# The fifteen middle passes of a fused transformer layer: a loop on the engines, or written out

## The chip, the cores and the metric

The kernel runs on one core of a Trainium2 chip. The metric is the time of one execution on the device, in microseconds (us), as the median of several runs.

## The reference

One pre-norm transformer layer on x of shape (16, 512, 256), f32, batch B = 16:

```
x = x + attn(layernorm(x))          # causal, ALiBi bias, 32 query heads, 16 key/value heads, head dim 64
x = x + ffn(layernorm(x))           # U1: 256->64, V1: 64->1024, gelu(tanh form) + b1, U2: 1024->64, V2: 64->256, + b2

qkv = x @ W_qkv                     # W_qkv (256, 4096)
scores = q @ k.T / 8 + slope * (pos_k - pos_q), masked where pos_q < pos_k
out = softmax(scores) @ v ; out @ W_out      # W_out (2048, 256)
```

## The kernel before

Every f32 product is made from f16 halves: a value is kept as hi + lo, and a product is three matmuls (lo times hi, hi times lo, hi times hi). Line numbers are those of the profile (L445 is the helper that issues nearly all matmuls).

**Tiling.** One batch element (512 tokens, 4 tiles of 128) is one unit of work. For it the kernel goes through 16 steps s, one for each key/value head, and each step has 5 segments n = 0 to 4. In each segment TensorE does a block of scores, a block of scores for the row maxima, and in fixed segments a projection of q, k or v, the product of probabilities and v (L445, o_acc), a piece of the output projection (proj from wo), transposes, and pieces of the feed-forward part.

**Stages.** The work of one head is spread over later steps: projections in step s, maxima 2 steps later, exponentials 7 later (ATT = 7), the product with v 8 later, the output projection 12 later, then the second layernorm and, in steps 13 to 15, the feed-forward part of the element before. So the body for index i holds the front of element i and the tail of element i - 1.

**Modes.** The body is a Python function that each engine builds for itself. It is built three times: as FIRST (i = 0, without the tail), as MID (i = 1 to 15, everything), and as LAST (i = 16, only the tail). FIRST and LAST are straight code with counts that are Python integers. MID is built once and stands in a loop on each engine (`eng.Fori(1, B)`, L340), run 15 times: 14 times the branch at its end is taken, once it falls through into LAST.

**Waits.** Engines are tied together only by semaphores that count up over the whole kernel and are never reset, so each wait needs a count that grows with i. A count is an object `Count`: i times a factor plus a constant. The function `at` turns it into what the wait takes: outside the loop an integer; in the loop a register. At the top of the loop each engine multiplies i by nine factors (`MULTIPLES`); where the constant isn't zero, `at` issues a `reg_add` on that engine right ahead of the wait (L327), into one register named target. There is no barrier between the engines at the loop's end: each has its own loop and its own branch, and only the counts hold them together.

**Order.** The order of each engine's instructions is written out by hand in tables (`FFN_PAIRS`, `X_PAIRS`, `U1_AT`, `LN2_AT` and so on). What stands around the end of a pass is, on TensorE: the last scores of step 15, the last maxima, the transposes of the next element's x (L462), the last product of the feed-forward part (`ffn_y`: proj from v_hi and h), then at the top of the next pass the first scores of step 0, maxima, transposes of o (L567). On ScalarE (ACT) p_hi (L696) and the exponentials p_f (L738); on GpSimd (POOL) p_lo = p_f - p_hi (L1090); on VectorE (DVE) the masked row maxima (L925), the hi/lo remainders (L851), and the sums into x_rows (L1032). SyncE (SP) issues the DMAs that copy the q and k halves into the layout the matmuls read, and those of x and of the result.

Of the kernel before, what the change touches and what calls it, by code (L numbers as in the profile page):

```python
# [154 lines left out]
MULTIPLES = (1, 2, 4, 8, 16, 32, 64, 80, 192)  # L155
# [4 lines left out]
FIRST, MID, LAST = "first", "mid", "last"  # L160
# [55 lines left out]
def layer(nc, x, w_qkv, w_out, u1, v1, b1, u2, v2, b2, k_aug, q_aug, ident_d, ident_b_d, causal_d, out):  # L216
    B = x.shape[0]
    ctx = ExitStack()
    with ctx:
# [115 lines left out]

        def iterations(name, eng, body):
            body(Count(0), FIRST)
            regs = {n: eng.alloc_register(f"{name}_{n}") for n in (*MULTIPLES, "target")}
            regs["eng"] = eng
            with eng.Fori(1, B) as i:  # L340
                for times in MULTIPLES:
                    eng.reg_mul(regs[times], i, times)
                body(Count(i, regs), MID)
            body(Count(B), LAST)


# [4 lines left out]
        def _(sp):  # L351
# [28 lines left out]
            def body(i, mode):  # L380
# [47 lines left out]
                if mode != FIRST:  # L428
                    sp.wait_ge(y_done, at(2 * i + FREE))
                    sp.dma_start(out[(i - 1).value()].rearrange("(t p) d -> p t d", p=P), x2[:, :, :]).then_inc(y_out, 16)  # L430

            iterations("sp", sp, body)
            sp.wait_ge(y_out, 16 * B + FREE)
            sp.wait_ge(x_in, 16 * (B + 1))
# [3 lines left out]
        def _(pe):  # L438
# [31 lines left out]
            def body(i, mode):  # L470
# [171 lines left out]
                for s in range(KV):  # L642
# [8 lines left out]
                    for n in range(SEG):  # L651
# [35 lines left out]
                        if (s, n) in U2_PAIRS and mode != FIRST:  # L687
                            ffn_u2(U2_PAIRS[s, n])

            iterations("pe", pe, body)  # L690


        @block.scalar
        def _(act):
# [30 lines left out]
            def body(i, mode):  # L725
# [39 lines left out]
                for s in range(KV):  # L765
# [3 lines left out]
                    for n in range(SEG):  # L769
# [67 lines left out]
                        if (s, n) in U1_AT and mode != FIRST:  # L837
# [4 lines left out]
                            copy(pp[0:RANK, t * P:(t + 1) * P], proj("p", t)[0:RANK, 0:P], 1.0 / FFN_SCALE).then_inc(hi_pp, 1)  # L842

            iterations("act", act, body)


# [331 lines left out]
```

## Time and profile before

| | us |
|---|---|
| median of 3 runs | 3042.26 (3040.5 to 3043.39) |
| profiled execution, its own time | 3041.37 |
| its span, from first to last instruction | 3039.6 |
| PE busy | 2813.3 (93%) |
| DVE busy | 2194.7 (72%) |
| ACT busy | 2190.9 (72%) |
| POOL busy | 1730.0 (57%) |

PE is TensorE's matmuls and PEld its weight loads; a busy share is of the span. Register, branch and semaphore instructions are not counted as busy, so the work that the loop itself makes shows only as idle time of the engines, put down to "issue" where no semaphore explains it, and in the answer for a source line, which counts such instructions too (PEldq, ACTq, DVEq, POOLq, SPq are the engines' sequencers).

### The profile page before, as it was taken

Reading aid. Unit: us, or ns where it says so; the run is one execution under the profiler, and the core shown is the slowest. Engines: PE = TensorE matmul, PEld = TensorE weight load, DVE = VectorE, ACT = ScalarE, POOL = GpSimd, SP = SyncE. Lnnn points to the kernel's source line nnn. Section 1 sums busy time; section 2 is a strip of 40 time slices with the busy share of each in tenths; the row PEclk is TensorE's granted clock in tenths of the full one; section 3 lists DMA queues with packets and bytes.
Section 4 is the critical chain, followed back from the end, with each engine's and each line's share of the span. In section 5 each row is a group of like instructions: output and inputs, shape, how many; then the busy total and the mean of one; then the engine's idle time right before and its main releaser. Section 6 shows DMA issues by size and latency. Waiting matters only on the chain.

```text
span 3039.6 us, 99681 instructions
## 1 busy us (share of the span) xinstructions
PE 2813.3 (93%) x32328; PEld 1966.0 (65%) x32328; DVE 2194.7 (72%) x6987; ACT 2190.9 (72%) x3892; POOL 1730.0 (57%) x1560
## 2 busy tenths in 40 slices
PE   4999999999989999999999999999899999999986
PEld 1666675766757666676666767667676666767664
DVE  6777677776767777677776777767677776777763
ACT  3767777777777777777777777777777777776783
POOL 1555565555655656555565665556555555565664
PEclk9999999999999999999999999999999999999998
DMA  5332232322223222232322323222232322323210
GB/s 169 68 72 58 63 71 46 79 58 69 62 55 77 53 72 60 56 76 49 78 58 60 73 47 79 55 72 60 56 75 50 77 59 56 73 48 82 55 35 8
DMA packets 220087, 195.25 MB, mean 64 GB/s; under 512 B 41738, under 2 KB 217866, under 8 KB 219274
## 3 DMA queue, kind: packets, MB, share of 16 engines
q1 hardware_dynamic: 219540, 188.32, 26.3%
q8 instruction: 299, 4.90, 0.7%
q14 instruction: 248, 2.03, 0.2%
HBM read 27.73 MB, written 8.39 MB: 12 GB/s over the span
## 4 chain that ended last, share of the span: by engine, by line
PE 31%; issue 27%; POOL 27%; ACT 5%; DVE 3%; POOLq 1%; ACTq 0%; DVEq 0%
POOL p_lo L1090 26%; PE proj L445 13%; PE scores L445 7%; PE o_acc L445 6%; PE max_scores L445 2%; PE ffn_acc L445 2%; ACT h_f L824 1%; ACT L738 1%; DVE v_lo L851 1%; ACT p_f L738 1%; ACT L824 1%; POOL h_lo L1113 1%; PE transposes L567 1%; DVE max_scores L925 1%; POOLq L327 1%
## 5 line engine op out<-in xcount | busy, mean ns | idle before, releaser
L1090 POOL TENSOR_TENSOR p_lo<-p_f,p_hi 128x512 f16<-128x512 f32 x1280 | 1476.6, 1158 | 1073.3 <-ACT p_hi L696 1070.8
L738 ACT ACTIVATE p_f<-scores 128x512 f32<-128x512 f32 x1280 | 756.4, 591 | 333.9 <-PE scores L445 211.5
L696 ACT ACTIVATE p_hi<-p_f 128x512 f16<-128x512 f32 x1280 | 802.3, 627 | 48.0 <-issue 33.7
L925 DVE CUSTOM_DVE_ANT_0 max_scores<-max_scores,causal 128x384 f32<-128x384 f32 (+3 forms) x1184 | 564.1, 508 | 274.6 <-PE max_scores L445 265.3
L445 PE MATMUL scores<-q_hi_lo,k_lo_hi 128*128 128x512 f16 (+3 forms) x2048 | 613.1, 300 | 28.4 <-issue 28.0
L445 PE MATMUL scores<-q_hi_aug,k_hi_aug 128*128 128x512 f16 (+3 forms) x2048 | 585.7, 299 | 0.0
L445 PE MATMUL o_acc<-v_hi_one,p_lo 128*128 128x65 f16 x5120 | 517.6, 194 | 13.7 <-POOL p_lo L1090 13.7
L445 PE MATMUL o_acc<-v_hi_one,p_hi 128*128 128x65 f16 x5120 | 517.9, 194 | 0.0
L445 PE MATMUL o_acc<-v_lo,p_hi 128*128 128x64 f16 x5120 | 517.7, 193 | 0.0
L445 PEld LDWEIGHTS o_acc<-v_hi_one,p_lo 128*128 128x128 f16 x5120 | 471.7, 98 | 49.7 <-issue 12.8
L445 PEld LDWEIGHTS o_acc<-v_lo,p_hi 128*128 128x128 f16 x5120 | 468.4, 98 | 19.5
L445 PEld LDWEIGHTS o_acc<-v_hi_one,p_hi 128*128 128x128 f16 x5120 | 468.6, 97 | 0.0
L445 PE MATMUL scores<-ident_bf,causal 128*128 128x128 bf16 x2048 | 448.0, 219 | 0.0
L925 DVE CUSTOM_DVE_ANT_0 ffn_acc<-ffn_acc,causal 128x384 f32<-128x384 f32 (+2 forms) x864 | 413.4, 509 | 26.3 <-PE ffn_acc L445 25.1
L445 PE MATMUL max_scores<-k_hi_aug,q_hi_aug 96*128 96x384 f16 (+3 forms) x1184 | 282.8, 300 | 52.1 <-DVE row_max L925 48.8
L445 PE MATMUL proj<-xn_t_hi,wqkv_lo 128*128 128x512 f16 x768 | 293.7, 382 | 28.8 <-DVE v_lo L851 27.3
L445 PE MATMUL proj<-xn_t_hi,wqkv_hi 128*128 128x512 f16 x768 | 292.8, 381 | 0.0
L445 PE MATMUL proj<-xn_t_lo,wqkv_hi 128*128 128x512 f16 x768 | 292.7, 381 | 0.0
L925 DVE DVE_READ_ACCUMULATOR2_ANT row_max<- 128x1 f32 x2048 | 284.4, 139 | 1.3
L445 PE MATMUL proj<-wo_hi,o_t_lo 128*128 128x256 f16 x1024 | 280.7, 274 | 2.6 <-DVE o_t_lo L851 1.5
L445 PE MATMUL proj<-wo_hi,o_t_hi 128*128 128x256 f16 x1024 | 280.3, 274 | 0.0
L445 PE MATMUL proj<-wo_lo,o_t_hi 128*128 128x256 f16 x1024 | 280.2, 274 | 0.0
(115 smaller groups left out, 5205.9 us busy)
## 6 DMA issues: line engine op xcount, KB each, us to landing
q_hi_aug<-q_pair_hi SPq DMA_DIRECT2D x512, 64.0 KB, 2.0
q_hi_lo<-q_pair_hi SPq DMA_DIRECT2D x512, 64.0 KB, 2.1
q_hi_lo<-q_pair_lo SPq DMA_DIRECT2D x512, 64.0 KB, 2.0
k_hi_aug<-k_pair_hi SPq DMA_DIRECT2D x256, 64.0 KB, 2.0
k_lo_hi<-k_pair_hi SPq DMA_DIRECT2D x256, 64.0 KB, 2.0
k_lo_hi<-k_pair_lo SPq DMA_DIRECT2D x256, 64.0 KB, 2.2
x_rows<-in_L_attn_inputs SPq DMA_DIRECT2D x17, 512.0 KB, 3.7
x_residual<-in_L_attn_inputs SPq DMA_DIRECT2D x16, 512.0 KB, 3.7
```

The source lines that it names most:

```text
L327: count.regs["eng"].reg_add(count.regs["target"], count.regs[count.times], count.plus)
L445: return nc.tensor.matmul(out_ap, lhs, rhs, start=start, stop=stop, skip_group_check=True)
L567: last = nc.tensor.transpose(bank[:, qt * P:(qt + 1) * P], o_f[:, qt, :], ident[:, :])
L696: return nc.scalar.activation(out_ap, in_ap, ACT.Copy, scale=scale)
L738: nc.scalar.activation(p_f[:, k % 3, :], score_bank[k % 2][:, :], ACT.Exp).then_inc(exp_done, 1)
L824: nc.scalar.activation(h_f[:, c % 2, :], proj("h", c)[:, :], ACT.Gelu_apprx_tanh, bias=b1c[:, c:c + 1], scale=1.0 / FFN_SCALE).then_inc(ge ...
L851: return nc.vector.scalar_tensor_tensor(out=out_ap, in0=bank, scalar=scale, in1=high, op0=ALU.mult, op1=ALU.subtract)
L925: last = nc.vector.tensor_tensor_reduce(out=bank, in0=bank, in1=causal[:, (T - 1 - qt) * P:S], scale=1.0, scalar=-3e38, op0=ALU.add, op1=A ...
L1090: nc.gpsimd.tensor_tensor(p_lo[:, slot, n, :], p_f[:, k % 3, :], p_hi[:, slot, n, :], ALU.subtract).then_inc(lo_p, 1)
L1113: nc.gpsimd.tensor_tensor(h_lo[:, c % 2, :], h_f[:, c % 2, :], h_hi[:, c % 2, :], ALU.subtract).then_inc(lo_h, 1)
```

## The change

The loop on the engines goes. The MID body is built fifteen times, one after the other, with i as a Python integer. `Count` then has no registers, so `at` gives an integer in each wait, no `reg_add` and no `reg_mul` is issued, and the addresses of the DMAs of x and of the result are constants. The order of the instructions in a body, the tiles and the semaphores stay as they are.

```diff
         def iterations(name, eng, body):
             body(Count(0), FIRST)
-            regs = {n: eng.alloc_register(f"{name}_{n}") for n in (*MULTIPLES, "target")}
-            regs["eng"] = eng
-            with eng.Fori(1, B) as i:
-                for times in MULTIPLES:
-                    eng.reg_mul(regs[times], i, times)
-                body(Count(i, regs), MID)
+            for i in range(1, B):
+                body(Count(i), MID)
             body(Count(B), LAST)
```

## Rows read from the trace of the kernel before

**Rows 1.** The page: its head, busy slices and granted clock.

```profile
PE 2813.3 (93%) x32328; PEld 1966.0 (65%) x32328; DVE 2194.7 (72%) x6987; ACT 2190.9 (72%) x3892; POOL 1730.0 (57%) x1560
...
PEclk9999999999999999999999999999999999999998
```

**Rows 2.** Waits of PE, whole span: total us, times, longest us.

```profile
PE max_scores L445 <- DVE row_max L925: 48.8, 39, 2.6
PE scores L445 <- issue: 28.0, 14, 2.4
PE proj L445 <- DVE v_lo L851: 27.3, 32, 1.2
```

**Rows 3.** Waits of PE in one pass, 723.5 to 907 us.

```profile
PE max_scores L445 <- DVE row_max L925: 2.7, 2, 1.4
PE scores L445 <- issue: 2.3, 1, 2.3
PE proj L445 <- DVE v_lo L851: 1.7, 2, 1.2
PE proj L445 <- DVE k_pair_lo L851: 1.2, 1, 1.2
PE proj L538 <- DVE v_lo L851: 0.8, 1, 0.8
PE proj L538 <- ACT h_f L824: 0.6, 1, 0.6
PE o_acc L445 <- POOL p_lo L1090: 0.4, 1, 0.4
PE proj L445 <- DVE x_acc L932: 0.3, 1, 0.3
```

**Rows 4.** Timeline around the third loop edge, PE, ACT, POOL, DVE: start, duration.

```profile
720.65 0.27 PE L445 MATMUL proj<-v_hi,h_hi 128*128 128x256 f16 x1
723.23 0.39 PE L445 MATMUL scores<-q_hi_lo,k_lo_hi 128*128 128x512 f16 x1 [2.30 <-issue]
...
719.65 0.60 ACT L696 ACTIVATE xn_t_hi<-transposes 128x512 f16<-128x512 f32 x1
722.77 0.63 ACT L696 ACTIVATE p_hi<-p_f 128x512 f16<-128x512 f32 x1 [2.52 <-issue]
...
723.47 1.16 POOL L1090 TENSOR_TENSOR p_lo<-p_f,p_hi 128x512 f16<-128x512 f32 x1 [4.78 <-ACT p_hi L696]
...
720.89 1.28 DVE L1032 SCALAR_TENSOR_TENSOR x_rows<-proj,x_rows 128x512 f32<-128x512 f32 x2
724.55 0.70 DVE L925 CUSTOM_DVE_ANT_0 max_scores<-max_scores,causal 128x512 f32<-128x512 f32 x1 [2.38 <-PE max_scores L445]
```

**Rows 5.** Line L340 (loop head and branch): count, min/median/max ns, first and last start.

```profile
L340 PEldq FUSED_REGOPS  x15: 84/84/88, 168.2 to 2747.6; - x15
L340 PEldq COMPARE_BRANCH  x15: 76/3684/4062, 350.5 to 2928.0; - x15
```

**Rows 6.** PE's timeline where the loop is left, after its 15th pass.

```profile
2929.74 0.27 PE L445 MATMUL proj<-v_hi,h_hi 128*128 128x256 f16 x1
2929.85 0.38 PE L445 MATMUL scores<-q_hi_lo,k_lo_hi 128*128 128x512 f16 x1
2930.06 0.22 PE L445 MATMUL scores<-ident_bf,causal 128*128 128x128 bf16 x1
2930.12 0.38 PE L445 MATMUL scores<-q_hi_aug,k_hi_aug 128*128 128x512 f16 x1
2930.34 0.38 PE L445 MATMUL max_scores<-k_hi_aug,q_hi_aug 96*128 96x512 f16 x1
2930.56 0.60 PE L567 MATMUL transposes<-ident,o_f 128*128 128x128 f32 x4
2930.99 0.38 PE L445 MATMUL scores<-q_hi_lo,k_lo_hi 128*128 128x512 f16 x1
```

**Rows 7.** PE's timeline: first scores of passes 2 and 15, each after a loop edge.

```profile
354.88 0.39 PE L445 MATMUL scores<-q_hi_lo,k_lo_hi 128*128 128x512 f16 x1 [2.35 <-issue]
...
2747.82 0.39 PE L445 MATMUL scores<-q_hi_lo,k_lo_hi 128*128 128x512 f16 x1 [2.28 <-issue]
```

**Rows 8.** PE's timeline where the loop is entered from FIRST.

```profile
169.44 0.38 PE L445 MATMUL scores<-q_hi_lo,k_lo_hi 128*128 128x512 f16 x1
...
170.28 0.39 PE L445 MATMUL max_scores<-k_hi_aug,q_hi_aug 96*128 96x512 f16 x1 [0.19 <-DVE row_max L925]
171.09 0.65 PE L567 MATMUL transposes<-ident,o_f 128*128 128x128 f32 x4 [0.43 <-DVE xn_t_lo L851]
```

**Rows 9.** Line L327 (the reg_add ahead of a wait), by engine.

```profile
L327 PEldq ALU_OP  x5445: 32/32/42, 168.6 to 2927.5; - x195
L327 ACTq ALU_OP  x5400: 35/35/38, 169.9 to 2928.2; - x193
```

**Rows 10.** Line L736 (a second wait, outside the loop only).

```profile
L736 ACTq EVENT_SEMAPHORE  x92: 17/17/17, 85.7 to 2981.2; - x92
```

**Rows 11.** PE's timeline: start of steps 13 and 14 in FIRST, 5 and 6 in pass 3.

```profile
136.92 0.38 PE L445 MATMUL scores<-q_hi_lo,k_lo_hi 128*128 128x512 f16 x1
...
146.80 0.38 PE L445 MATMUL scores<-q_hi_lo,k_lo_hi 128*128 128x512 f16 x1
...
590.00 0.38 PE L445 MATMUL scores<-q_hi_lo,k_lo_hi 128*128 128x512 f16 x1
...
599.87 0.38 PE L445 MATMUL scores<-q_hi_lo,k_lo_hi 128*128 128x512 f16 x1
```

**Rows 12.** DMA queues in one pass, 539.64 to 724 us: packets, MB, share.

```profile
q8 instruction: 18, 0.29, 0.7%
q14 instruction: 16, 0.13, 0.2%
```

## The prediction

> **What bounds the kernel now.** I read the page first, then the waits of PE, then the timeline where a pass of the loop ends, then the two source lines that the loop makes (L340, L327), which the page doesn't count as busy. The page shows PE busy for 93% of the span, every other engine at 72% or less, and a granted clock of nine tenths or more, so the 2.4 GHz level, in nearly all slices [rows 1]. PE sets the pace, and what counts is what its idle time waits for. In the list of its waits one entry belongs to no engine: 28.0 us in 14 times, put down to issue, ahead of the first scores of a pass [rows 2]. Fourteen is the number of times that the loop's branch is taken. In a single pass that wait is there once (2.3 us), beside 7.7 us of waits for DVE, ACT and POOL, about ten of them (2.7 + 1.7 + 1.2 + 0.8 + 0.6 + 0.4 + 0.3) [rows 3].
>
> The timeline shows the edge itself [rows 4]. PE's last matmul of the pass starts at 720.65 and the first of the next at 723.23. ACT stands still for 2.52 us at the same place, also with issue named, and POOL and DVE then wait for these two. Nothing in the data holds PE there: the scores follow at once where the loop is left. L340 says what does: PE's compare-and-branch takes 3684 ns as a median and 76 ns at the least, the one time that it falls through [rows 5]. PE has matmuls queued when its sequencer stands at the branch, which is why 3.7 us of branch leave some 2.0 us of idle PE.
>
> **The change, part by part.**
>
> *The branch.* It goes, 14 times. What comes in its place is the code as it now runs from pass 15 into LAST: the last projection at 2929.74, the scores at 2929.85, 0.11 us later, and then maxima, transposes and the next scores at 2930.34, 2930.56 and 2930.99 with no wait named before any of them [rows 6]. That is the closest row to what every edge becomes, and it has the same feed-forward tail before it. Two ways to price the 14 edges. By the idle row: 28.0 us. By the length of passes: from the first scores of pass 2 (354.88) to those of pass 15 (2747.82) are 13 passes with an edge each, (2747.82 - 354.88) / 13 = 184.07 us; from there to the first scores of LAST (2929.85) is one pass without a taken edge, 182.03 us [rows 7 and 6]. The difference is 2.04 us, and 14 x 2.04 = 28.6 us. I take 28.6.
>
> *What is late next.* In the gap DVE does its last two sums into x_rows, 720.89 to 722.17 [rows 4], and the next pass's second block of maxima and its q projection wait for them. Without the edge PE starts the scores at about 720.76. In the exit the second scores start 1.14 us after the first and are some half a microsecond long [rows 6], so PE comes to these maxima about 1.6 us after 720.76, at 722.4: after DVE, by 0.2 us. ACT can do p_hi at 720.25 instead of 722.77, when its last copy ends, and POOL follows it. So I take no new wait. The other end is the entry from FIRST, also without an edge ahead: there DVE and the o transposes are late by 0.19 and 0.43 us as named [rows 8], and that pass lasts 354.88 - 169.44 = 185.44 us against 184.07, so 1.37 us more [rows 7 and 8]. FIRST ends without the feed-forward tail, which is PE's time for the others to catch up, so it is the farther row; I keep 14 x 1.37 = 19.2 us as the upper price of a give-back.
>
> *The register instructions.* 5445 of them on PE at 32 ns and 5400 on ACT at 35 ns [rows 9], and in each pass the multiplications at the top, behind the branch (the fused pair on PE takes 84 ns) [rows 5], which lies inside the edge that I have priced. If every reg_add of PE stood bare on its path it would be 5445 x 0.032 = 174 us. It doesn't: steps that do the same in FIRST, with constants, and in the loop, with registers, take the same time, 146.80 - 136.92 = 9.88 us for step 13 of FIRST and 599.87 - 590.00 = 9.87 us for step 5 of pass 3 [rows 11]. Where PE has matmuls queued the sequencers' work is hidden by them, and a step is unchanged to 0.01 us, over 240 steps at most 2.4 us either way. What is left are the ten waits of a pass outside the edge, where PE has run dry and the chain over ACT or DVE counts. A reg_add of about 35 ns in it goes, but where it also carried a first wait, a semaphore instruction stands in its place (17 ns on ACT [rows 10]). Say 18 ns net for each of ten waits: 0.18 us a pass, 2.7 us in 15. The ends are nothing (or 2.4 us lost), and three instructions of 35 ns in each wait with nothing in their place, 10 x 3 x 0.035 x 15 = 15.8 us. I take 3 us, near the lower end because the semaphore instruction is the near row.
>
> *Fetching the longer program.* I take nothing. One pass already brings 18 and 16 packets of instructions over its two queues [rows 12]: the body is fetched afresh in every pass, so writing it out fetches the same amount, in order. Within a pass PE has no wait for issue but the one at the edge [rows 3].
>
> At this place the Trainium skill bears on the sum twice. "Runtime: NRT & Kernel Launch", section on instruction fetch mechanics, says that fetching in order is mostly hidden and that a taken branch to a place out of the buffered window stalls; this trace agrees, with 3684 ns for the taken branch and 76 ns for the other. "Advanced Engine Details and Errata", section Control Flow Timing, gives a compare-and-branch about 108 ns; by that figure 14 branches would be an estimated 1.5 us, and the trace's 28.0 us would have to be something else.
>
> *The DMAs.* SP issues the same ones, with constant addresses. It isn't waited for by PE in a pass [rows 3], so no gain and no loss.
>
> **Sum.** 3041.37 - 28.6 - 3 = 3009.8 us for the profiled execution. It is 0.9 us below the median of the runs (3042.26), so about 3010.5 for a median; I say 3010.
>
> **The rivals.** A measurement of this kernel can tell about 0.2% (6 us) from no change.
>
> - *Give-back at the seam.* The edge goes, but it has been the pause in which DVE and ACT caught up, and PE waits for them in step 0 as at the entry: 28.6 - 19.2 = 9.4 us, and 3 for the registers: 3042.3 - 12.4 = 3030. For it: the entry rows. Against it: the exit, which has no such wait, and the 0.2 us that I find in hand.
> - *The stall isn't the branch.* Some other thing between passes costs the 2 us and stays (a wait across engines that the trace can't see); then only the branch's own 76 ns and the registers go: 14 x 0.076 + 3 = 4 us, 3038. For it: issue only means that nothing visible explains it. Against it: two engines stop at once, the minimum of 76 ns is the fall-through, and PE flows on there.
> - *Slower: straight code comes late.* Fetching 15 bodies in order misses now and then, each miss at the price of an edge, 2.0 us of idle PE. There are 18 packets on the larger queue in a pass, 270 in 15. If one in ten missed, 27 x 2.0 = 54 us: 3042 - 32 + 54 = 3064. It decides from 32 / 2.0 = 16 misses on. For it: a loop could prefetch something a long program doesn't. Against it: inside the pass the same 18 packets come with no such wait.
> - That the change doesn't do what it says I leave at nothing: with integers `at` can't issue a register instruction.
>
> **How the numbers follow.** My forecast 85%, the give-back 8%, the stall that isn't the branch 4%, slower 3%. The forecast itself runs from 2998 (15.8 for the registers instead of 3) to 3016 (2.4 lost there instead of 3 won). The give-back lies at 3030; I go a part of the way to it, to 3020, since a small give-back of 0.3 us an edge (4 us) is within what I can't exclude, and leave its full size outside. Faster by over 0.2%: the forecast and the give-back, 0.93; the same, 0.04; slower, 0.03.
>
> **What would show it.** The trace after should have no register or branch instruction on the five queues but a last one of SP; no wait of PE for issue at the first scores of a pass; p_hi of ACT at the seam without its 2.5 us; passes of 181.5 to 182.1 us from first scores to first scores. Step 5 of a pass should stay at 9.87 us. The waits of PE outside the edge should stay near 7.7 us a pass, and a little less would be the register part. The prediction is wrong if waits for DVE or ACT of a microsecond stand in step 0 of each pass (give-back), or if waits for issue of about 2 us are strewn over the passes (fetching).

## The result and the profile after

| | before | after |
|---|---|---|
| median, us | 3042.82 | 3003.11 (3001.69 to 3005.99) |
| ratio to before | | 0.9865, 95% interval 0.9853 to 0.9877 |
| profiled execution, us | 3041.37 | 3001.69 |
| its span, us | 3039.6 | 2999.9 |
| instructions in the trace | 99681 | 85467 |

The kernel is 1.35% faster, 39.7 us. I forecast 3010 (2998 to 3020). (The median before is now one of four runs, hence 3042.82 and not 3042.26.) The first lines of the page after answer to [rows 1]:

```profile
span 2999.9 us, 85467 instructions
...
PE 2804.2 (93%) x32328; PEld 1970.4 (66%) x32328; DVE 2203.5 (73%) x6987; ACT 2194.3 (73%) x3892; POOL 1726.2 (58%) x1560
...
q8 instruction: 257, 4.21, 0.6%
q14 instruction: 151, 1.24, 0.1%
```

The same 32328 matmuls; PE's busy time is 9.1 us less (0.3%) and its idle time 30.6 us less. The two queues that bring instructions carried 257 and 151 packets. PE's waits over the whole span, to set beside [rows 2] (us in total, times, longest):

```profile
PE max_scores L441 <- DVE row_max L921: 52.6, 40, 2.7
PE proj L441 <- DVE v_lo L847: 27.3, 32, 1.2
PE proj L441 <- DVE k_pair_lo L847: 18.5, 15, 1.2
```

The entry "PE scores <- issue: 28.0, 14" is gone and has no successor. (Lines after are 4 lower than before: L441 is L445, L921 is L925.) The timeline at the seam of passes 3 and 4, as in [rows 4]: start, duration, for PE, then ACT, POOL and DVE.

```profile
712.65 0.27 PE L441 MATMUL proj<-v_hi,h_hi 128*128 128x256 f16 x1
712.76 0.38 PE L441 MATMUL scores<-q_hi_lo,k_lo_hi 128*128 128x512 f16 x1
713.90 0.38 PE L441 MATMUL scores<-q_hi_lo,k_lo_hi 128*128 128x512 f16 x1
...
711.65 0.60 ACT L692 ACTIVATE xn_t_hi<-transposes 128x512 f16<-128x512 f32 x1
712.14 0.62 ACT L692 ACTIVATE p_hi<-p_f 128x512 f16<-128x512 f32 x1
713.45 0.60 ACT L734 ACTIVATE p_f<-scores 128x512 f32<-128x512 f32 x1 [0.68 <-PE scores L441]
...
712.84 1.16 POOL L1086 TENSOR_TENSOR p_lo<-p_f,p_hi 128x512 f16<-128x512 f32 x1 [2.22 <-ACT p_hi L692]
...
712.89 1.28 DVE L1028 SCALAR_TENSOR_TENSOR x_rows<-proj,x_rows 128x512 f32<-128x512 f32 x2
714.08 0.69 DVE L921 CUSTOM_DVE_ANT_0 max_scores<-max_scores,causal 128x512 f32<-128x512 f32 x1
```

From the last projection to the scores it is 0.11 us, from these to the second scores 1.14, both as at the exit in [rows 6]. ACT's p_hi follows its copy at once. DVE's sums end at 714.17, and PE doesn't wait for them. Last, the first scores of passes 1, 2 and 15 and of LAST, as in [rows 6 to 8]:

```profile
166.90 0.38 PE L441 MATMUL scores<-q_hi_lo,k_lo_hi 128*128 128x512 f16 x1
...
349.69 0.38 PE L441 MATMUL scores<-q_hi_lo,k_lo_hi 128*128 128x512 f16 x1
...
2709.99 0.38 PE L441 MATMUL scores<-q_hi_lo,k_lo_hi 128*128 128x512 f16 x1
...
2891.53 0.38 PE L441 MATMUL scores<-q_hi_lo,k_lo_hi 128*128 128x512 f16 x1
```

(2709.99 - 349.69) / 13 = 181.56 us a pass, against 184.07. I call the stretch from the first scores of pass 1 to those of LAST the middle: it holds all fifteen passes and nothing else. It took 2929.85 - 169.44 = 2760.4 us before and 2891.53 - 166.90 = 2724.6 after, 35.8 less. The other 3.9 us of the span went outside it: 2.5 before 166.90, 1.4 after 2891.53.

### The profile page after: what moved, and what is told of

Its sections match the earlier page's. It is cut to its first block, busy times and chain, and to the rows that moved or that the text cites. A ratio compares the mean times of both kernels' runs of the same rounds, so it can differ in the third digit from the quotient of the medians.

```text
span 2999.9 us, 85467 instructions
## 1 busy us (share of the span) xinstructions
PE 2804.2 (93%) x32328; PEld 1970.4 (66%) x32328; DVE 2203.5 (73%) x6987; ACT 2194.3 (73%) x3892; POOL 1726.2 (58%) x1560
## 4 chain that ended last, share of the span: by engine, by line
PE 77%; DVE 6%; ACT 5%; issue 3%; POOL 3%; DMA 0%; DVEq 0%; POOLq 0%; ACTq 0%; SPq 0%
PE proj L441 31%; PE scores L441 19%; PE o_acc L441 14%; PE max_scores L441 5%; PE ffn_acc L441 5%; PE transposes L563 3%; DVE max_scores L921 2%; POOL h_lo L1109 1%; POOL p_lo L1086 1%; ACT L734 1%; ACT h_f L820 1%; DVE v_lo L847 1%; ACT p_f L734 1%; PE proj L534 1%; DVE ffn_acc L921 1%
## 5 line engine op out<-in xcount | busy, mean ns | idle before, releaser
L921 DVE CUSTOM_DVE_ANT_0 max_scores<-max_scores,causal 128x384 f32<-128x384 f32 (+3 forms) x1184 | 564.3, 508 | 244.4 <-PE max_scores L441 231.5
L441 PE MATMUL scores<-q_hi_lo,k_lo_hi 128*128 128x512 f16 (+3 forms) x2048 | 613.1, 300 | 2.5 <-DMA q_hi_aug<-neg_max_t_lo 2.2
L441 PE MATMUL scores<-q_hi_aug,k_hi_aug 128*128 128x512 f16 (+3 forms) x2048 | 585.9, 299 | 0.0
L441 PE MATMUL o_acc<-v_hi_one,p_lo 128*128 128x65 f16 x5120 | 517.9, 194 | 9.9 <-POOL p_lo L1086 9.9
L441 PE MATMUL o_acc<-v_hi_one,p_hi 128*128 128x65 f16 x5120 | 517.9, 194 | 0.0
L441 PE MATMUL o_acc<-v_lo,p_hi 128*128 128x64 f16 x5120 | 517.9, 193 | 0.0
L441 PEld LDWEIGHTS o_acc<-v_hi_one,p_lo 128*128 128x128 f16 x5120 | 471.5, 98 | 46.3 <-POOL p_lo L1086 19.9
L441 PEld LDWEIGHTS o_acc<-v_lo,p_hi 128*128 128x128 f16 x5120 | 468.5, 98 | 19.5
L441 PEld LDWEIGHTS o_acc<-v_hi_one,p_hi 128*128 128x128 f16 x5120 | 468.7, 97 | 0.0
L441 PE MATMUL scores<-ident_bf,causal 128*128 128x128 bf16 x2048 | 448.0, 219 | 0.0
L921 DVE CUSTOM_DVE_ANT_0 ffn_acc<-ffn_acc,causal 128x384 f32<-128x384 f32 (+2 forms) x864 | 413.3, 508 | 29.5 <-PE ffn_acc L441 27.7
L441 PE MATMUL max_scores<-k_hi_aug,q_hi_aug 96*128 96x384 f16 (+3 forms) x1184 | 282.1, 299 | 56.9 <-DVE row_max L921 52.6
L441 PE MATMUL proj<-xn_t_hi,wqkv_lo 128*128 128x512 f16 x768 | 293.1, 382 | 28.8 <-DVE v_lo L847 27.3
L441 PE MATMUL proj<-xn_t_lo,wqkv_hi 128*128 128x512 f16 x768 | 292.3, 381 | 0.0
L441 PE MATMUL proj<-xn_t_hi,wqkv_hi 128*128 128x512 f16 x768 | 292.1, 380 | 0.0
L921 DVE DVE_READ_ACCUMULATOR2_ANT row_max<- 128x1 f32 x2048 | 283.4, 138 | 1.3
L441 PE MATMUL proj<-wo_hi,o_t_lo 128*128 128x256 f16 x1024 | 280.4, 274 | 1.5 <-DVE o_t_lo L847 1.5
L441 PE MATMUL proj<-wo_hi,o_t_hi 128*128 128x256 f16 x1024 | 280.0, 273 | 0.0
L441 PE MATMUL proj<-wo_lo,o_t_hi 128*128 128x256 f16 x1024 | 279.9, 273 | 0.0
```

Source lines behind the costliest of these rows:

```text
L441: return nc.tensor.matmul(out_ap, lhs, rhs, start=start, stop=stop, skip_group_check=True)
L921: last = nc.vector.tensor_tensor_reduce(out=bank, in0=bank, in1=causal[:, (T - 1 - qt) * P:S], scale=1.0, scalar=-3e38, op0=ALU.add, op1=A ...
```

## The experiments

The kernels that were run together share a chip and their own runs of the kernel before, and those medians differ (3042.8, 3044.6, 3046.2, 3045.7 us). So each kernel has its ratio here, and the middle, which repeats to 0.2 us (the kernel after was run twice: 2724.6 and 2724.8). What lies outside the middle doesn't repeat so well.

| kernel | median, us | ratio (95%) | middle, us | rest of the span, us |
|---|---|---|---|---|
| before | 3042.8 | 1 | 2760.4 | 279.2 |
| after | 3003.1 | 0.9865 (0.9853 to 0.9877) | 2724.6 | 275.3 |
| written out, registers kept | 3007.7 | 0.9879 (0.9864 to 0.9894) | 2730.2 | 273.0 |
| loop with a hint | 3016.4 | 0.9906 (0.9891 to 0.9921) | 2730.1 | 281.6 |
| loop over three bodies | 3022.8 | 0.9927 (0.9913 to 0.9940) | 2740.8 | 279.5 |
| PE alone written out | 3015.0 | 0.9902 (0.9887 to 0.9917) | 2736.3 | 274.7 |
| all but PE written out | 3043.0 | 0.9986 (0.9977 to 0.9995) | 2763.6 | 273.4 |
| after, ACT's waits swapped | 3009.1 | 0.9879 (0.9864 to 0.9895) | 2729.1 | 277.6 |
| after, once more | 3005.6 | 0.9870 (0.9855 to 0.9885) | 2724.8 | 277.4 |
| after, no gate at the maxima | 2996.5 | 0.9835 (0.9821 to 0.9848) | 2715.5 | 280.4 |
| the same once more | 2993.3 | 0.9829 (0.9815 to 0.9842) | 2715.4 | 277.6 |
| and two more hops of DVE | 2994.7 | 0.9830 (0.9816 to 0.9843) | 2714.4 | 278.1 |

The second tool is the length of each step, from the first scores of a step to those of the next, median over passes 1 to 15. Steps 1 to 7, 9, 11 and 12 are equal to 0.02 us in the first six kernels of this table (step 5, for one: 9.87 before and after, 763.88 to 773.75 in the trace after). The others:

```
us                              step 0    8     10     13     14     15
before                           9.89  10.45  12.05  14.53  17.32  14.48  (12.34 the once no branch is taken)
written out, registers kept      9.88  10.45  12.05  14.53  17.32  12.34
loop with a hint                 9.88  10.45  12.05  14.53  17.32  12.34
PE alone written out            10.42  10.28  11.98  14.53  17.39  12.41
all but PE written out           9.89  10.45  12.04  14.45  17.14  14.61
after                            9.88  10.28  11.96  14.45  17.22  12.40
after, ACT's waits swapped       9.88  10.28  11.96  14.51  17.45  12.41
after, no gate at the maxima     9.88  10.13  11.94  14.44  17.21  12.32
```

**Registers kept, branch gone.**

```diff
-            with eng.Fori(1, B) as i:
-                for times in MULTIPLES:
-                    eng.reg_mul(regs[times], i, times)
+            for i in range(1, B):
+                for times in MULTIPLES:
+                    eng.reg_mov(regs[times], i * times)
                 body(Count(i, regs), MID)
```

> Fifteen passes written out, but every wait still takes its count from a register: reg_add stays ahead of the waits, and nine reg_mov stand at the top of a pass in place of the multiplications. Only the branch is gone. Theory (the branch is worth 2.1 us at each of 14 edges, 29.4 us, and the register instructions some 6.5 us spread over the waits in which PE has run dry): 3042.8 - 29.4 = 3013 us, no PE wait for issue at the first scores, steps 8, 10, 13 and 14 of a pass as long as before (10.45, 12.05, 14.53, 17.32 us). Rival (the branch is all, and the 6.5 us are other things of a straight program): 3003 to 3005 us and the shorter steps of the kernel after.

Measured: the middle 2897.29 - 167.14 = 2730.2 us, 30.3 less than before; only step 15 changed. So the branch is 30.3 us of the 35.8 in the middle and the registers 5.5. The median, 3007.7, is below the 3013 expected; in the profiled executions the rest of the span was 6.2 us shorter than that of before, which the theory hadn't. For the passes, the theory holds and the rival falls. The first scores of pass 1 and the entry to LAST:

```profile
167.14 0.38 PE L445 MATMUL scores<-q_hi_lo,k_lo_hi 128*128 128x512 f16 x1
...
2897.29 0.38 PE L445 MATMUL scores<-q_hi_lo,k_lo_hi 128*128 128x512 f16 x1
```

**The loop with a hint for its branch.**

```diff
-            with eng.Fori(1, B) as i:
+            with nc.Fori(1, B, engines=bass.OrderedEngineSet([eng.engine]), hint_back_edge=True) as i:
```

> The loop stays with its registers; each engine gets one instruction at the top of a pass that announces the loop's branch, so that the first instructions of the loop can be fetched before the branch is taken. Theory (what the edge costs is fetching the top of the body): the edges fall to some tenths of a us, 3013 to 3017 us. Rival (the branch empties the sequencer whatever is fetched): 3042 us, with 2 us of PE waiting for issue at each of 14 edges.

Measured: 3016.4 us, and the middle, 2901.45 - 171.38 = 2730.1, is that of the written-out kernel with registers to 0.1 us. The loop's line on PE, as in [rows 5] (count, min/median/max ns), and the seam:

```profile
L340 PEldq BRANCH_PREFETCH_HINT  x15: 36/36/45, 170.1 to 2718.5; - x15
L340 PEldq COMPARE_BRANCH  x15: 88/963/1423, 352.4 to 2899.6; - x15
```

The same branch takes 963 ns as a median instead of 3684, and PE has enough matmuls queued to cover that: no wait for issue stands at the scores any more. What cost 2.1 us at an edge was waiting for the instructions of the loop's top, neither the branch as such nor the registers set behind it. That is what the Trainium skill says ("Runtime: NRT & Kernel Launch", instruction fetch mechanics). The 108 ns of its other page, "Advanced Engine Details and Errata", section Control Flow Timing, are near the 76 and 88 ns of the one branch that falls through; none of TensorE's taken branches came near, with 3359 to 4062 ns before and still 743 to 1423 with the hint.

The hint gave back the edges, but its kernel as a whole is 8.7 us slower than the written-out one with registers (3016.4 against 3007.7, both on one chip). In the profiled executions 8.6 us of that stand in the rest of the span, ahead of pass 1 and from LAST to the end. Another 2.2 us stand outside the span: the whole time exceeds it by 4.0 to 4.3 us in each of this kernel's four executions and by about 1.8 in those of the others. No run here tells why.

**A loop over three bodies.**

```diff
-            with eng.Fori(1, B) as i:
+            with eng.Fori(1, B - 2, 3) as i:
                 for times in MULTIPLES:
                     eng.reg_mul(regs[times], i, times)
-                body(Count(i, regs), MID)
+                for k in range(3):
+                    body(Count(i, regs, plus=k), MID)
```

> Five trips of a loop over three bodies, registers in every wait: 4 taken branches instead of 14. Theory (each taken branch costs the same, however long the body): 3042.8 - 10 x 2.1 = 3022 us. Rival (the edge costs more with a longer body, or once a kernel): over 3030 or near 3042.

Measured: 3022.8 us, and PE waits for issue at the scores 4 times, 8.6 us in all:

```profile
533.57 0.38 PE L446 MATMUL scores<-q_hi_lo,k_lo_hi 128*128 128x512 f16 x1
717.66 0.39 PE L446 MATMUL scores<-q_hi_lo,k_lo_hi 128*128 128x512 f16 x1 [2.03 <-issue]
```

(Seams without and with a taken branch.) An edge costs about the same behind a body three times as long, 2.15 us of idle PE against 2.0 before. Over the kernel with no branch the middle is 10.6 us longer, 2.7 an edge, not 2.1; the difference is told at the end.

**PE alone written out, and all but PE.** `iterations` asks for `name == "pe"` (or `!=`) and gives that side the straight passes with constants, the other the loop.

> TensorE's passes are written out with constants, the other four engines keep the loop and the registers. Theory (every engine stops at its own branch, and ACT's stop of 2.5 us then holds PE through p_lo): PE runs on over the seam, but stands later in step 0 at the product with v; about half of the edge is won, 3042.8 - 14 x 1.1 - 1 = 3026 us. Rival (only PE's branch counts, because it is the bound): 3012 us.

> The complement of the run before: TensorE alone keeps the loop and the registers, the other four engines are written out with constants. Theory (PE's own branch stops it for 2.1 us, whatever the others do; the short hops on ACT, DVE and POOL come back): 14 edges stay, the steps 8, 10, 13, 14 shorten in part, a pass with an edge of 183.6 to 183.9 us, 3035 to 3040 us. Rival (the stops of the engines add up, each with a share): under 3030 us.

Measured: 3015.0 us for PE alone, so between theory (3026) and rival (3012), much nearer to the rival. ACT still stops at each of its 14 edges (p_hi <- issue, 32.4 us), and PE stands only 0.5 us longer in step 0, where I had expected about 1:

```profile
717.94 0.63 ACT L700 ACTIVATE p_hi<-p_f 128x512 f16<-128x512 f32 x1 [2.61 <-issue]
...
719.86 0.20 PE L449 MATMUL o_acc<-v_hi_one,p_lo 128*128 128x65 f16 x1 [0.70 <-POOL p_lo L1094]
```

Between the scores of step 0 and this product PE has maxima, transposes and the q projection to do, about 3 us, and most of ACT's stop passes behind them. The complement gains next to nothing: 3043.0, ratio 0.9986, with PE's 14 waits for issue (28.9 us) all there. So it is PE's own branch that the 2 us hang on. My 3035 to 3040 was too low: three edges of this kernel were followed by a stretch at the lower clock, 5 us in all (last section), and without them its middle would be some 1.7 us shorter than that of before. The steps tell whose registers they were. Steps 8 and 10 shorten (by 0.17 and 0.07 to 0.09) when PE has constants and don't when only the others have; steps 13 and 14 (0.08 and 0.10 in the kernel after) when the others have and not when only PE has. That is 0.26 us a pass of PE's own and 0.18 of the others'; step 15 is 0.06 longer in the kernel after, which leaves 0.38. The shares aren't clean, since PE alone also made step 14 longer (17.39) and the others alone made it shorter than both together (17.14 against 17.22).

PE's own part can be read off step 8 in pass 3, where the product with v waits for p_lo of POOL. The two lines in the kernel before, then in the kernel after:

```profile
621.09 1.16 POOL L1090 TENSOR_TENSOR p_lo<-p_f,p_hi 128x512 f16<-128x512 f32 x1
622.49 0.19 PE L445 MATMUL o_acc<-v_hi_one,p_lo 128*128 128x65 f16 x1 [0.40 <-POOL p_lo L1090]
```

```profile
613.45 1.16 POOL L1086 TENSOR_TENSOR p_lo<-p_f,p_hi 128x512 f16<-128x512 f32 x1
614.66 0.20 PE L441 MATMUL o_acc<-v_hi_one,p_lo 128*128 128x65 f16 x1 [0.22 <-POOL p_lo L1086]
```

PE starts 0.24 us after the end of p_lo with registers and 0.06 with constants, and so in all fifteen passes; FIRST, which has constants in either kernel, has 0.06 in both. In the trace before, a reg_add waits for p_lo's semaphore, and a semaphore instruction stands between it and the weight load; in the trace after, the weight load waits for that semaphore itself. The 0.18 us between the two is what step 8 became shorter by.

**The waits of ACT swapped.**

```diff
+                    if count - back + 1 > 0:
+                        act.wait_ge(lo_p, at(count - back + 1))
                     act.wait_ge(pe_scores, at(count + 1))
-                    if count - back + 1 > 0:
-                        act.wait_ge(lo_p, at(count - back + 1))
```

and alike for q_hi, k_hi, v_hi and gelu.

> The kernel after, with the two waits ahead of ACT's exponentials, of q_hi, k_hi, v_hi and of the gelu in the other order, so that the wait for TensorE, which comes last, no longer sits on the compute instruction but on a semaphore instruction ahead of it. Theory (what the constants won in a pass, 0.4 us, is that the late semaphore releases the compute instruction itself, not a register instruction and then the compute instruction): most of the 0.4 us a pass is lost again, steps 8, 10, 13, 14 go back toward 10.45, 12.05, 14.53, 17.32 us, 3007 to 3010 us. Rival (it is the number of sequencer instructions that counts, which stays as it is in this kernel): no change, 3003 us.

Measured: the middle 4.4 us longer (2729.1 against 2724.7), with not an instruction more. Steps 13 and 14 became 0.06 and 0.23 longer, where the other engines' part lies, and step 14 longer even than before (17.45 against 17.32); steps 8 and 10, PE's, stayed, against what I had written: PE's own waits, which weren't touched here, set them. Of two waits in a row the first written sits on the compute instruction, the second on a semaphore instruction ahead of it. The hop, the time from the last matmul that an instruction needs to its start, can be read off one k projection, PE's last matmul and ACT's copy of it, in the kernel before and then after:

```profile
678.82 0.38 PE L445 MATMUL proj<-xn_t_hi,wqkv_hi 128*128 128x512 f16 x1
...
679.31 0.60 ACT L696 ACTIVATE k_pair_hi<-proj 128x512 f16<-128x512 f32 x1 [0.78 <-PE proj L445]
```

```profile
852.46 0.38 PE L441 MATMUL proj<-xn_t_hi,wqkv_hi 128*128 128x512 f16 x1
...
852.87 0.60 ACT L692 ACTIVATE k_pair_hi<-proj 128x512 f16<-128x512 f32 x1 [0.70 <-PE proj L441]
```

0.49 us before, 0.41 after; over the k projections of passes 2 to 15 the medians are 0.49 and 0.42, and 0.48 with the waits swapped. Before, the late wait sat on the reg_add for the second wait, and ACT could start the copy only behind it.

**No gate ahead of the maxima.**

```diff
                     dve.wait_ge(pe_max, at(SEG * g + n + 1))
-                    dve.sem_inc(gate, 1)
```

> The kernel after without the increment of the semaphore gate ahead of the row maxima (nobody waits for it), so that DVE's wait for TensorE sits on the maximum itself and 1280 semaphore instructions of DVE go. Theory (a late wait on the compute instruction itself is some 0.08 us faster; PE waits for row maxima about 2.9 us in a pass): 0.1 to 0.4 us a pass, 2997 to 3001 us. Rival (DVE is not what the end hangs on at these places, or the maximum takes the same time to start): 3003 us.

Measured: 2996.5 us, the middle 9.3 us shorter than the kernel after's, more than the 6 us that I had given as the most. A hop of this kind is longer than ACT's. Last matmuls and first maximum, kernel after and then without gate:

```profile
725.57 0.38 PE L441 MATMUL max_scores<-k_hi_aug,q_hi_aug 96*128 96x384 f16 x2
726.14 0.57 DVE L921 CUSTOM_DVE_ANT_0 max_scores<-max_scores,causal 128x384 f32<-128x384 f32 x1 [0.49 <-PE max_scores L441]
```

```profile
726.65 0.38 PE L441 MATMUL max_scores<-k_hi_aug,q_hi_aug 96*128 96x384 f16 x2
727.08 0.57 DVE L920 CUSTOM_DVE_ANT_0 max_scores<-max_scores,causal 128x384 f32<-128x384 f32 x1 [0.34 <-PE max_scores L441]
```

0.57 us against 0.43, so 0.14 a hop. The gain lies in steps 8, 11 and 12 (0.15 each, about one hop) and in step 15 (0.08). The edit shortens the hop and takes out 1280 semaphore instructions at once, and no run tells the two apart; that each of the three steps gained one hop speaks for the hop. Whether the same edit would help with counts in registers wasn't tried.

> The kernel after once more, beside these three on the same chip: 3003 us by every theory; passes of 181.53 us. It also tells whether its first scores at 76.5 us (80.0 before) and the 108.3 us from the last pass to the end (109.7 before) come with the kernel or with the run: the same values within 0.5 us if with the kernel, values anywhere between 76 and 81 and between 105 and 111 if with the run.

Measured: 3005.6 us, passes of 181.55; first scores at 77.9 us (76.5 in the other run), 109.2 us from LAST to the end (108.3). So both differ by more than half a microsecond in one kernel: the run decides over a microsecond or two of them. The first W_qkv load landed 9.6 us after its issue in this run and 8.1 in the other, and the granted clock behind LAST was 0.86 against 0.88.

**Two more hops of DVE,** the gates at both `bn_aggr` gone and in `normalise` the wait for the reciprocal written ahead of that for PE.

> The kernel without gate ahead of the maxima, and two more hops of DVE shortened: no gate ahead of the bn_aggr of either layernorm, and the product o_f carries the wait for its reciprocal itself (the wait for TensorE, long over, moves to the semaphore instruction). Theory (each late wait on the compute instruction itself saves some 0.08 us where PE hangs on DVE): up to 0.2 us a pass below 180.97, 1 to 3 us below the kernel without gate, 2993 to 2996 us. Rival (PE hangs on none of these): the same as the kernel without gate, 2996.5 us.

> The kernel without gate ahead of the maxima once more, beside the one with the further hops, on the same chip: 2996.5 us and passes of 180.97 us by every theory.

Measured: the middle 2714.4 against 2715.4 us, 1.1 less, all in step 15; the medians, 2994.7 and 2993.3, can't tell the two apart. Either is faster than both kernels of this case; the one without the gate at the maxima, a single edit, is the version to keep: ratio 0.983 to before, about 0.3% under the kernel after.

## Why the prediction was right

For the profiled execution I had 3009.8 us and it took 3001.69, 8.1 less: 1.7 from the branch, 2.5 from the registers and 3.9 from the ends.

*The branch, 28.6 us: measured 30.3.* The mechanism is as put: 14 edges, gone whole, and each seam now looks like the exit. The size was 1.7 short. The exit pass that I took as the pattern (182.03 us) had 0.13 us in step 6 that most others didn't (9.14 against 9.01; three more had 9.06 to 9.23); the written-out kernel with registers has 181.91, and (184.07 - 181.91) x 14 = 30.2.

*What is late next: nothing, as I had it.* Pass 1 alone has 10.8 to 10.9 us in step 0 in the kernel after, and 9.9 in all later passes; entering it costs the same in every kernel. So the give-back belongs to the entry; that the missing feed-forward tail of FIRST makes it fits, but no run tried it. The 0.2 us in hand for DVE's sums sufficed: they end at 714.17, and PE comes to the maxima behind the second scores at 714.39, 0.2 us later.

*The registers, 3 us: measured 5.5.* This is the term that I mis-sized, by half. That they cost nothing where PE has matmuls queued was right (step 5: 9.87 and 9.87), and PE's waits outside the edge fell from 7.7 to 7.5 us in a pass (I had counted about ten of them; [rows 3] has nine). In the waits I counted the reg_add's own 35 ns against a semaphore instruction's 17, 18 ns net. What counts is on which instruction the late semaphore sits: where it sits on the compute instruction itself, that starts 80 ns sooner on ACT and 180 ns sooner at PE's product in step 8, and the trace after has the waits in that order without anyone having asked for it. I also put the cost into the chains over ACT and DVE, while steps 8 and 10 shorten only with PE's own constants.

*Fetching the longer program: nothing, as I had it, but it isn't the same amount.* The larger queue before and in the written-out kernel with registers, to set beside the 257 packets after:

```profile
q8 instruction: 299, 4.90, 0.7%
q8 instruction: 275, 4.51, 0.7%
```

This queue is TensorE's: it has 257 packets with PE alone written out and 299 in the complement. So 24 packets went with the 14 edges and 18 with the register instructions. With the hint it has 286.

*The ends, put at nothing: measured 3.9 us.* No step of mine speaks of them. The two W_qkv loads landed 2.0 us earlier (8.1 and 12.6 us from issue against 10.1 and 14.6), and from LAST to the end PE's granted clock was 0.88:

```profile
2891.53:2999.85 108.32, 78.67 (x926) 0.88 0.03 11
```

(length, PE busy, granted clock), against 109.65 us at 0.86 before, and 105.86 at 0.91 with the registers kept. The middle alone would have made 3041.37 - 35.8 = 3005.6 of the profiled execution. Of these 3.9 us some 2 may be luck of the profiled execution: the second run of the kernel after had 277.4 us there, only 1.8 less than before. The rest of the span runs from 273.0 to 281.6 us over all kernels, with 2 and 3 us between two runs of one kernel. The first load landed 8.1 to 10.6 us after its issue, and by 8.1 and 9.6 in the two runs of the kernel after, so this is at least in part the run's; what sets it stays open.

Of the rivals, the give-back and slow fetching are refuted by the seam and by the passes of 181.5 us; that the stall wasn't the branch, by the kernel that loses only the branch and by the hint.

## What to carry to other kernels

A loop on the engines with a body as long as this one, some 4400 instructions of TensorE, pays for fetching its top at every taken branch, here 3.7 us of TensorE's sequencer and 2.1 us of the kernel; a short body wasn't tried. Write the passes out, or give the branch a hint, which is one argument and got all of it back in the passes, though here the kernel as a whole stayed 8.7 us behind the written-out one. What constants add over registers is small, 5.5 us here, and sits in the waits in which the bounding engine has run dry. There, write the wait that comes last so that it lands on the compute instruction, and put no semaphore instruction between them: 0.08 us a hop on ScalarE, 0.14 on VectorE, 0.18 at one product of TensorE. Nine microseconds in all came from one deleted line on VectorE.

## What the runs showed of the hardware beyond that

A taken branch can cost more than its stall. In the kernel with PE alone looping, three of the edges were followed by a fall of TensorE's granted clock from 2.4 to 1.2 GHz, and step 0 took 11.5 to 11.6 us instead of 9.89 there; one of the four edges of the loop over three bodies did the same. PE had stood idle for 2.28, 2.30 and 2.05 us ahead of the three, but two other edges of that kernel, with 2.41 and 2.51 us, had no fall, and neither had those of [rows 4] and [rows 7], with 2.28 to 2.35; so the length of the idle time alone doesn't tell, and what does stays open. The two stretches right behind an edge, with and without the fall (length, PE busy, granted clock, DMA share, GB/s):

```profile
536.70:540.70 4.00, 3.98 (x16) 0.62 0.39 133
722.20:726.20 4.00, 3.95 (x46) 1.00 0.40 135
```

16 matmuls against 46 in the same 4 us. It is 1.6 to 1.7 us each time, 5 us in that kernel, and is why its passes came out longer than before's. In the kernel before none of the 14 edges had it in the profiled execution, and no kernel in which PE doesn't stand idle at an edge had such a fall between pass 1 and LAST; so a loop whose edges leave TensorE idle is also exposed to this.
